# Four tiles of a masked graph attention take their row and column term through VectorE and an f32 identity matmul

## What is computed

```python
# layer 0: graph attention
h = relu(layernorm(x))
scores = (h @ W @ a1)[:, None] + (V @ W @ a2)[None, :]
e = where(scores > 0, scores, 0.2 * scores)
e = where(adj > 0, e, -9e15)
x = x + elu(softmax(e, axis=1) @ V + h)
# layer 1: sums over neighbours
h = relu(layernorm(x))
x = x + relu((adj.T @ h) @ U.T / adj.sum(axis=0)[:, None])
```

## Time and profile before

| | |
|---|---|
| median of 3 runs | 372.39 us |
| the profiled execution | 372.29 us, of which its span is 370.5 us |
| PE matmul busy | 308.6 us (83%) |
| DVE busy | 301.3 us (81%) |
| ACT busy | 257.2 us (69%) |
| POOL busy | 117.6 us (32%) |
| mean granted TensorE clock | 0.959 |

### The profile page before, as it was taken

The page is one execution under the profiler, slowest core; times in us unless marked ns, Lnnn a source line. Parts: engine busy times, 40 slices in busy tenths (PEclk is TensorE's granted clock), DMA queues, the critical chain, the costliest instruction groups (busy, mean ns, idle before and its releaser), DMA issues.

```text
span 370.5 us, 15390 instructions
## 1 busy us (share of the span) xinstructions
PE 308.6 (83%) x7126; PEld 278.3 (75%) x7126; DVE 301.3 (81%) x410; ACT 257.2 (69%) x323; POOL 117.6 (32%) x120
## 2 busy tenths in 40 slices
PE   1816676668878877989898999999989999999995
PEld 0712555557667766877788999888989999999995
DVE  7889999889799749999987779999988876402965
ACT  2310799779999879999989899997797786101000
POOL 8856398288250383030107103003102010401000
PEclk9956699869999999999999999999999999999999
DMA  9999999999999999999201002000010113510211
GB/s 163 140 109 108 108 109 109 138 107 107 110 109 143 104 107 106 105 101 104 70 4 35 25 25 82 25 25 23 21 46 25 46 27 66 117 34 2 57 34 30
DMA packets 28822, 27.83 MB, mean 75 GB/s; under 512 B 22265, under 2 KB 24121, under 8 KB 28758
## 3 DMA queue, kind: packets, MB, share of 16 engines
q0 software_dynamic: 4752, 16.90, 43.9%
q1 hardware_dynamic: 21846, 9.39, 10.6%
q10 hardware_dynamic: 2160, 0.56, 0.9%
HBM read 74.08 MB, written 3.43 MB: 209 GB/s over the span
## 4 chain that ended last, share of the span: by engine, by line
PE 34%; DVE 31%; issue 11%; ACT 10%; POOL 7%; DMA 6%; SPq 0%; POOLq 0%; DVEq 0%; ACTq 0%
DVE scratch L899 22%; PE w L1252 12%; PE q L1339 9%; PE q L1225 7%; PE w L1339 5%; DVE arena L951 4%; ACT q L749 4%; DMA adj_sb<-in_adj_dram 4%; POOL adj_sb L464 4%; ACT arena L735 3%; ACT arena L731 3%; DMA bi<-rows_sb 2%; POOL adj_sb L468 1%; POOL buf_b L521 1%; PE w L1298 1%
## 5 line engine op out<-in xcount | busy, mean ns | idle before, releaser
L1252 PE MATMUL w<-v_sb,arena 128*64 128x65 f32 (+1 forms) x4224 | 158.3, 226 | 1.3 <-ACT arena L735 1.1
L899 DVE CUSTOM_DVE_ANT_0 scratch<-adj_sb,t_row 125x2048 uint8<-125x2048 uint8 x66 | 153.5, 2325 | 3.0 <-DMA adj_sb<-in_adj_dram 1.7
L1252 PEld LDWEIGHTS w<-v_sb,arena 128*64 128x64 f32 (+1 forms) x4224 | 140.5, 139 | 9.2 <-ACT arena L735 2.1
L1225 PE MATMUL q<-bi,adj_sb 128*64 128x125 bf16 (+1 forms) x1664 | 93.2, 225 | 32.0 <-ACT q L749 25.4
L1225 PEld LDWEIGHTS q<-bi,adj_sb 128*64 128x64 fp8e4 (+1 forms) x1664 | 67.9, 109 | 47.2 <-ACT q L749 35.4
L731 ACT ACTIVATE arena<-q,t_col 128x1000 f32<-128x1000 f32 (+2 forms) x102 | 88.1, 868 | 5.4 <-PE q L1225 5.3
L735 ACT ACTIVATE arena<-arena,t 128x1000 f32<-128x1000 f32 (+2 forms) x58 | 63.6, 1097 | 17.8 <-DVE arena L951 17.0
L951 DVE SCALAR_TENSOR_TENSOR arena<-arena,b_col,q 128x1000 f32<-128x1000 f32 (+1 forms) x43 | 52.3, 1224 | 14.1 <-PE q L1225 9.4
L749 ACT ACTIVATE q<-second_row,minus_b 128x750 f32<-128x750 f32 (+1 forms) x49 | 47.9, 977 | 1.1
L749 ACT ACTIVATE q<-arena,minus_b 128x375 f32<-128x375 f32 (+1 forms) x53 | 42.3, 800 | 1.3
L1339 PE MATMUL q<-g_all,adj_sb 124*128 124x129 f16 (+1 forms) x588 | 34.8, 220 | 0.0
(11 more groups left out here) (144 smaller groups left out, 236.2 us busy)
## 6 DMA issues: line engine op xcount, KB each, us to landing
adj_sb<-in_adj_dram POOLq DMA_DIRECT2D x33, 500.0 KB, 40.4
saved_dram<-x_sb SPq DMA_DIRECT2D x6, 193.5 KB, 2.9
t_row<-saved_dram SPq DMA_DIRECT2D x6, 193.5 KB, 2.5
arena<-s_dram SPq DMA_DIRECT2D x2, 500.0 KB, 7.3
out_dram<-v_sb SPq DMA_DIRECT2D x10, 96.0 KB, 1.8
x_sb<-in_x_dram SPq DMA_DIRECT2D x1, 928.0 KB
v_sb<-x_dram SPq DMA_DIRECT2D x1, 768.0 KB, 5.6
v_sb<-n_L_gnn_entity_embs_dram ACTq DMA_DIRECT2D x2, 256.0 KB, 5.7
```

Source lines behind the costliest of these rows:

```text
L899: nc.vector.tensor_tensor_reduce(out=junk[0:R, :], in0=adj_bytes[0:R, b, half], in1=t_row[0:R, half], scale=1.0 / ONE, scalar=0.0, op0=ALU ...
L1225: last = nc.tensor.matmul(q[n % Q_SLOTS][e:e + width, bank, start:start + R], weights, bi[:, i % BI_SLOTS, k, :], start=not ON_ACT[n] and ...
L1252: last = nc.tensor.matmul(att(i)[e0:e1, bank, place_in, :], e[:, k * R + e0:k * R + e1], v_sb[:, c, :], start=(c == 0 and place_in == 0), ...
```

## The change

In tiles 8, 13, 18 and 23 of group 1 (`ON_PE`) the relu on ACT is gone. DVE makes max(row term, column term) with one `tensor_scalar` from SBUF to SBUF (`leak`), into the last 250 columns of the three slots of `arena`, which group 1 leaves free. PE adds it into a fresh `q` by four f32 matmuls against the 128 x 128 identity (250, 125, 125 and 250 columns), ahead of the masks. The exponential takes another bias, `t02`. The piece is issued on DVE five tiles ahead (`PE_LEAD`), at the start of the step of tiles 3, 8, 13 and 18. There is one buffer for it, so all but the first wait for the masks of the previous such tile. The row's next DMA on SP waits for `leaked` too.

```diff
+    PE_GROUP = 1
+    PE_TILES = (8, 13, 18, 23)
+    PE_LEAD = 5
+    ON_PE = [i == PE_GROUP and c in PE_TILES for i, c in TILES]
+    ON_ACT = [c not in DVE_TILES[i] and not (i == PE_GROUP and c in PE_TILES) for i, c in TILES]
...
+        def leak_pieces():
+
+            return arena[:, 0:E_SLOTS, 750:1000]
...
+                    sp.wait_ge(leaked, leaks_to(NC * (i - 1)))
...
+                if ON_PE[n]:
+                    act.wait_ge(masked, n + 1)
+                    nc.scalar.activation(e_part(n, nb), part(q[n % Q_SLOTS], nb), ACT.Exp, bias=t02[:, c:c + 1])\
+                        .then_inc(exped, 1)
+                    return
...
-                if n >= Q_SLOTS and ON_ACT[n - Q_SLOTS]:
+                if n >= Q_SLOTS and from_psum(n - Q_SLOTS):
                     act.wait_ge(exped, n - Q_SLOTS + 1)
...
+            def leak(n, i, c):
+
+                done = leaks_to(n)
+                if done == 0:
+                    wait_for_row(dve, i)
+                    dve.wait_ge(t_scaled, 3)
+                else:
+                    dve.wait_ge(masked, max(k for k in range(n) if ON_PE[k]) + 1)
+                row = a_rows[i % 2][:, 0:750].rearrange("p (s c) -> p s c", s=E_SLOTS)
+                nc.vector.tensor_scalar(leak_pieces(), row, b_col[:, c:c + 1], None, ALU.max).then_inc(leaked, 1)
...
             for n, (i, c) in enumerate(TILES):
-                if not ON_ACT[n]:
+                if n + PE_LEAD < len(TILES) and ON_PE[n + PE_LEAD]:
+                    leak(n + PE_LEAD, *TILES[n + PE_LEAD])
+                if not ON_ACT[n] and not ON_PE[n]:
                     scores(n, GROUPS[i][1] - GROUPS[i][0], i, c)
...
                 again = not ON_ACT[n] and nb < 8
+                if ON_PE[n]:
+                    pe.wait_ge(leaked, leaks_to(n + 1))
+                    for bank, start, s, s0, s1 in ((0, 0, 0, 0, 250), (0, 250, 1, 0, 125), (1, 0, 1, 125, 250), (1, 125, 2, 0, 250)):
+                        nc.tensor.matmul(q[n % Q_SLOTS][:, bank, start:start + s1 - s0], ident[:, :], leak_pieces()[:, s, s0:s1],
+                                         start=start == 0, stop=False)
```

More of the change, by code:

```diff
@@ L59, in graph_layers_kernel @@
                  (0, 1, 2, 3, 4, 5, 6, 7, 8, 10, 11, 12, 13, 14, 15, 16, 17, 18, 19, 20, 21, 22, 23, 24, 25, 26, 27, 28, 29, 30, 31)]
-    ON_ACT = [c not in DVE_TILES[i] for i, c in TILES]
+    PE_GROUP = 1
[3 more added lines that the diff above has]
+    ON_ACT = [c not in DVE_TILES[i] and not (i == PE_GROUP and c in PE_TILES) for i, c in TILES]
     GUARD_TILES = [(4, 8, 10, 11, 11, 15, 15, 18, 18, 19, 20, 24),
@@ L239, in graph_layers_kernel @@
         h1_done = sem("h1_done")
+        leaked = sem("leaked")
         h1_weighted, s_done = sem("h1_weighted"), sem("s_done")
@@ L329, in sums_to, with leaks_to, from_psum @@
         def sums_to(n):
-            return n - sum(ON_ACT[:n])
+            return n - sum(ON_ACT[:n]) - sum(ON_PE[:n])
         def relus_to(n):
             return sum(ON_ACT[:n])
+        def leaks_to(n):
+            return sum(ON_PE[:n])
+        def from_psum(n):
+            return ON_ACT[n] or ON_PE[n]
+        def leak_pieces():
+            return arena[:, 0:E_SLOTS, 750:1000]
         def at(what, i, c):
@@ L746, in relu @@
                     act.wait_ge(r1_ready, 1)
-                if c == min(k for k in range(NC) if k not in DVE_TILES[i]):
+                if c == min(k for k in range(NC) if ON_ACT[i * NC + k]):
                     wait_for_row(act, i)
@@ L948, in scores @@
                     wait_for_row(dve, i)
+                if c == min(DVE_TILES[i]):
                     dve.wait_ge(t_scaled, 3)
@@ L1209, in mask @@
                     pe.wait_ge(relued, relus_to(n + 1))
-                elif n >= Q_SLOTS and ON_ACT[n - Q_SLOTS]:
+                elif n >= Q_SLOTS and from_psum(n - Q_SLOTS):
                     pe.wait_ge(exped, n - Q_SLOTS + 1)
@@ L1225, in mask @@
                         last = nc.tensor.matmul(q[n % Q_SLOTS][e:e + width, bank, start:start + R], weights, bi[:, i % BI_SLOTS, k, :],
-                                                start=not ON_ACT[n] and start == 0, stop=ON_ACT[n] or (closes and not again),
+                                                start=not from_psum(n) and start == 0, stop=ON_ACT[n] or (closes and not again),
                                                 skip_group_check=ON_ACT[n])
```

## The result

The changed kernel takes 379.49 us in the median of four executions (378.32 to 380.49) against 372.39 before (372.35 to 373.3). The profiled execution took 379.88 us with a span of 378.0, so 7.59 and 7.5 us more than before.

What follows compares the result with a forecast made beforehand. DVE was taken to bound the end of group 1, ACT 0.86 us behind. 4.16 us at `spread` plus 1.58 for the pieces of tiles 18 and 23 gave 5.74; 372.29 + 5.74 = 378.0 us, range 375.2 to 379.5.

Steps and rivals of the forecast that it cites:

- The wait at tile 13 and its place: PE at tile 13 of group 1 idles 3.7 us until DVE's piece, started at 103.38 us, ends at 104.17.
- The piece: Each of DVE's four added `tensor_scalar` of 128 x 750 takes 0.79 us, at 0.83 ns per column.
- Rival 1: DVE's piece runs at two elements per cycle, 0.56 us: S is 5.05, kernel 377.3 us; chance 0.32.
- The clock: After PE's idle time at tile 13 the clock falls to 1.2 GHz for 4.1 us, until 108.3.
- Rival 2: The clock stays at 2.4 GHz at tile 13: S is 4.2, kernel 376.5 us; chance 0.15.
- The identity: PE's f32 identity matmuls at tile 13 take 2.39 us at the low clock, 1.26 at the full one.
- The exponential of 13 and `spread`: ACT's exponential of tile 13 starts 5.28 us late, at 107.68; DVE's `spread`, awaiting ACT's squares, 4.16 late, at 112.28.
- ACT's gain: Without the relu, two tile steps on ACT take 3.22 us in place of 3.46: 0.24 gained per tile.
- rival 5: Faster: ACT sets the end of group 1, four times 0.24 us counts, kernel 371.3 us; chance 0.04.
- S: Shift of DVE's score of tile 25, end of group 1: 5.74 us, moving the rest of the kernel equally.
- Rival 3: Long low-clock spell at tile 13, piece 0.99 us, identity 3.0 us: S is 7.4, kernel 379.7 us; chance 0.08.
- Rival 4: The stall is absorbed by slack at the start of group 2: no change, 372.3 us; chance 0.04.

Runs made afterwards that it cites:

- change_again: The changed kernel run once more, unaltered, for more executions and a second trace: 378.84 us, ratio 1.0174 to the kernel before.
- only_13: The changed kernel with only tile 13 going the new way, in place of 8, 13, 18 and 23: 379.03 us, ratio 1.0188.
- early_all: The changed kernel with all pieces two tiles earlier in DVE's list (`PE_LEAD` 7 for 5): 376.16 us, ratio 1.0103.
- filled: The changed kernel with 64 bf16 matmuls, later overwritten, on PE ahead of the identity matmuls of tile 13: 378.31 us, ratio 1.0152.
- without_13: The changed kernel with only tiles 8, 18 and 23 going the new way: 375.33 us, ratio 1.0072.
- in_the_gap: The changed kernel with only tiles 8 and 13, the piece of 13 made behind the guards of tile 4: 372.83 us, ratio 1.0012.
- piece_shapes: The kernel before with three extra `tensor_scalar` probes on DVE (2 rows of 125, 3 rows of 125, one row of 124): 372.05 us, one execution.
- elu_later: The kernel before with `elu`, which waits for POOL's sum, moved from tile 4 to 6 in DVE's list: 373.17 us, ratio 1.0017.
- elu_later_two: As elu_later, with tiles 8 and 13 the new way, their pieces in the steps of tiles 3 and 7: 373.15 us, ratio 1.0018.
- after: The changed kernel as first measured and traced, against the kernel before: median 379.49 us, ratio 1.0185; profiled execution 379.88 us.

## Why the prediction was right

- **The time.** The median lies 1.49 us above the forecast of 378.0 and 0.01 below the end of the range. Two of the four executions (379.88 and 380.49) lie outside it, change_again gave 378.84. That the median fell inside is luck. The chain of waits is not: each of its steps up to the score of tile 25 stands in the trace, 0.4 to 0.6 us later than put.
- **The wait at tile 13 and its place.** Right: idle 3.90 us for 3.7, released by the piece of 103.31. only_13 has the whole stall alone, early_all takes it away by two tiles in DVE's list.
- **The piece.** The wrong price: 0.99 us (0.90 to the next start) for 0.79, so the upper bound, taken from the score of the same size, was the true one. The step that failed is the slope through operations of 8 and 128 columns, which this shape does not follow. Rival 1 fell too (0.56 us). Two of the probes run at the rate of its rule. The Trainium skill (VectorE: DVE Perf Modes, What auto-detection actually checks) also asks that the outermost dimensions of source and destination be both even or equal. Here the destination has three rows, and the source is 750 columns in one run. If it is taken as one run, the condition is not met, and 0.99 us agrees; no run here separates an odd number of rows from an unequal one.
- **The clock.** Right: 1.2 GHz from 104.4 until just before 108, so about 3.5 us for 4.1. Rival 2 fell. By filled the clock costs 1.6 us up to the exponential (1.3 for change_again, where it is 3.37 us from the identity on), which is also the difference between the forecast (107.68) and rival 2 (106.1). Most of tile 13's work lay in the spell in either case, so the shorter spell gave nothing back.
- **The identity.** It took 2.62 us for 2.39 (1.40 for 1.26 at full clock): eight records of 250 and 125 columns cost more than the price per column of long ones says. The low price was also badly founded. The row at 10.21, from which its 1.59 ns per column come, was read as one at the low clock, but the window of PE before gives a grant of 1.00 there:

```profile
10.20:13.70 3.50, 3.48 (x19) 1.00 1.20 162
```

  Its price is nearly twice the 0.84 of the full clock, so the low clock is likely, but no row shows it. The rows that stand at 0.50 gave 2.0 ns, that is 3.0 us, and the 2.62 measured lies between. That 2.39 came so near is in part luck. In change_again the grant fell some 0.4 us after the first record, and the identity took 2.28.
- **The exponential of 13 and `spread`.** 5.71 late for 5.28: PE starts 0.24 later than put, mostly by the dearer piece, the identity is 0.23 longer, and the masks give 0.04 back. `spread` 4.61 for 4.16, waiting 3.84 us: the mechanism as put.
- **ACT's gain.** The step "3.22 in place of 3.46" failed. 3.46 runs from exponential to exponential, 3.22 was counted from the start of the masks, which lies 0.12 later (90.42 against 90.30), and the identity was 0.14 short. Measured: 90.30 to 93.76, 3.46 us, in which a wait of 0.89 stands where the relu did. The gain is zero, which the sum did not need, but rival 5 did.
- **The score of tile 25.** 6.38 late for 5.74: 0.45 from `spread`, and two pieces at 0.90 for 0.79, 0.22. Counted from the end of DVE's wait for POOL's sum, the pieces behind it cost 0.86 each in early_all and 0.88 in without_13.
- **From there on.** That S moves the rest of the kernel by S was nearly right: the first mask of group 2 came 6.83 late, and group 2 took 0.72 more, partly at the low clock. The sum put these 1.17 us at nothing. Together with the 0.64 at tile 25 they are 1.8 of the 1.9 us by which the profiled execution lies above the forecast; the median lies 0.4 lower. change_again has 0.09 of the 1.17 and no fall of the clock in group 2. What decides between the two isn't shown, nor whether the same remainder stands in only_13's executions without a trace.
- **Rivals 3, 4 and 5.** Rival 3 had the piece, but not the identity of 3.0 us; its 379.7 lies near the result only because the remainder, which it doesn't have, came on top. Rival 4 fell, as group 3 starts 7.55 late. Rival 5 fell twice: with the stall gone (early_all) the kernel is 3.8 us slower, and with the pieces in gaps as well (in_the_gap) nothing is gained.

Open: what the slower executions of only_13 did, and what makes the clock fall at the start of group 2; a piece written as two rows of 375, which by the probes would take some 0.6 us (an estimate from the slope of 0.56 ns), wasn't tried. By in_the_gap it could only make the loss smaller.

## What to carry to other kernels

A lead counted in list positions is no lead in time: ask when the engine that makes the operand reaches it, and when the other wants it. A removed instruction pays only if its successor's input is there earlier; here the exponential found PE's longer work in the place of its relu. Where two engines ended a stage within a microsecond, moving work between them gave nothing, and the stall of PE cost its own length and then 1.6 us by the clock.

## What was not expected of the hardware

- A `tensor_scalar` in f32 ran at one column per 1.04 ns with a destination of three rows, and at about one per 0.56 ns with two rows or one (piece_shapes, each shape once).
- A POOL sum of 0.54 us took 2.40 us beside a guard of DVE (elu_later), and a guard of 2.29 us took 2.51 beside the end of the sum (elu_later_two).
- Around 2 us of idle time the clock at the start of group 2 went either way. It fell after 1.97, 2.04, 2.06 and 2.24 us (elu_later, without_13, elu_later_two, after) and stayed at full after 2.12 us (early_all), 1.95 us (filled) and shorter ones. With the fall group 2 was longer by 0.4 to 1.4 us: by 1.4 where its first masks were already slow (elu_later, elu_later_two), by 0.4 and 0.7 where the clock fell a microsecond or so later (without_13, after). So such a boundary can't be foretold from the idle time alone. Not every longer group 2 is the clock's: in in_the_gap it lasted 63.74 us at full clock, with a `bi` DMA of 2.34 us at its end for 1.75 before.
- One execution of elu_later took 962.55 us, the others at most 374.01. No trace covers it.
